# TensorE's semaphore increments in a graph-and-experts kernel: from the matmul itself to a drain behind it

## The reference, cut to what matters

```python
x = layernorm(x)                                  # 6250 x 256
agg_in  = segment_sum((x @ W_in.T + b_in)[src], dst) / max(cnt_dst, 1)
agg_out = segment_sum((x @ W_out.T + b_out)[dst], src) / max(cnt_src, 1)
gi = concat(agg_in, agg_out) @ W_ih.T + b_ih
gh = x @ W_hh.T + b_hh
r, z = sigmoid(gi_r + gh_r), sigmoid(gi_i + gh_i)
n = tanh(gi_n + r * gh_n)
x1 = x_raw + (1 - z) * x + z * n
x2 = x1 + sum over the two best experts of weight * MLP_e(layernorm(x1))
```

## Time and profile before

| | |
|---|---|
| time, median of 3 runs | 3089.86 us (3088.94 to 3093.74) |
| span of the profiled execution | 4434.5 us |
| TensorE matmuls busy in it | 2745.1 us, 62% |
| VectorE, ScalarE, GpSimd busy | 47%, 20%, 49% |
| mean granted TensorE clock | 0.808 of full |

### The profile page before, as it was taken

How to read it: one execution, slowest core, us unless ns; L and a number is a source line. 1 busy time by engine, 2 the same in 40 slices (tenths; PEclk the granted TensorE clock), 3 DMA queues, 4 the chain that set the end, 5 groups by cost and what they waited for, 6 DMA issues and landing times. The chain is left out here.

```text
span 4434.5 us, 68226 instructions
## 1 busy us (share of the span) xinstructions
PE 2745.1 (62%) x14312; PEld 1616.8 (36%) x14313; DVE 2093.1 (47%) x6910; ACT 908.1 (20%) x1572; POOL 2164.5 (49%) x2165
## 2 busy tenths in 40 slices
PE   5211159977777777777764555555555555566896
PEld 2100025533333333333322333333333333345775
DVE  8201179975565556655552333443333433354221
ACT  4100026631112111111110010110111101112443
POOL 0777700035665555655645444444444444433786
PEclk9655589988888888888877777777777777787998
DMA  3100000022222222222222222222222222212444
GB/s 116 30 24 24 18 16 0 0 95 80 86 81 82 78 79 81 79 83 81 84 72 83 77 82 72 74 79 74 83 72 76 75 75 82 71 60 45 80 80 61
DMA packets 178175, 298.24 MB, mean 67 GB/s; under 512 B 51779, under 2 KB 123460, under 8 KB 178118
## 3 DMA queue, kind: packets, MB, share of 16 engines
q0 software_dynamic: 106560, 234.06, 19.8%
q10 hardware_dynamic: 44790, 35.90, 2.6%
q1 hardware_dynamic: 26768, 27.70, 2.0%
HBM read 255.56 MB, written 41.94 MB: 67 GB/s over the span
## 5 line engine op out<-in xcount | busy, mean ns | idle before, releaser
L431 POOL DMA_INDIRECT ring<-split_rows,live x782 | 791.5, 1012 | 923.4 <-DVE live L1035 381.8
L431 POOL DMA_INDIRECT over<-split_rows,gather_row x782 | 747.5, 956 | 933.0 <-PE bank L1674 681.5
L1600 PE MATMUL bank<-over,over 128*128 (+1 forms) x4920 | 1008.9, 354 | 143.1 <-issue 123.6
L1600 PEld LDWEIGHTS bank<-over,over 128*128 (+1 forms) x4920 | 485.9, 102 | 597.7 <-issue 351.9
L974 DVE TENSOR_SCALAR over<-iota_cols,live,live 128x128 f16 x1564 | 411.4, 319 | 119.9 <-issue 113.1
L392 POOL DMA_INDIRECT list<-sort,sort x336 | 332.7, 990 | 218.3 <-issue 111.0
L1674 PE MATMUL bank<-ring,dense 128*128 x980 | 329.5, 430 | 126.7 <-issue 100.1
L1714 PE MATMUL bank<-dense,dense 128*128 128x512 f32 (+1 forms) x600 | 262.0, 437 | 184.5 <-DVE dense L1183 174.1
L1675 PE MATMUL bank<-ones_col,dense 128*128 128x1 f16 x1960 | 334.9, 171 | 2.7 <-issue 2.5
L1674 PE MATMUL bank<-over,dense 128*128 x980 | 277.7, 386 | 94.5 <-issue 77.8
L614 ACT ACTIVATE over<-live,live 128x788 f16 x245 | 221.6, 945 | 492.2 <-remote 271.7
(11 more groups left out here) (304 smaller groups left out, 3927.7 us busy)
## 6 DMA issues: line engine op xcount, KB each, us to landing
norm<-in_x SPq DMA_DIRECT2D x20, 640.0 KB
ring<-split_rows,live POOLq DMA_INDIRECT x782
over<-split_rows,gather_row POOLq DMA_INDIRECT x782
split_rows<-over SPq DMA_DIRECT2D x10, 640.0 KB
in_edge_means<-dense ACTq DMA_DIRECT2D x50, 128.0 KB
dense<-in_x ACTq DMA_DIRECT2D x50, 128.0 KB
dense<-in_edge_means ACTq DMA_DIRECT2D x50, 128.0 KB
out<-dense ACTq DMA_DIRECT2D x25, 256.0 KB
```

The source lines that it names most:

```text
L431: g.indirect_dma_start(out=rings[d][:, i % ring_slots[d], :], out_offset=None, in_=table[:], in_offset=bass.IndirectOffsetOnAxis(ap=gather ...
L1600: ins = t.matmul(bank[h][:, 0:HS + 1], rows_(half), slots(h), start=False, stop=False, skip_group_check=True)
```

## The change

Every increment by TensorE in the ranking, the visits and the dense stage (1386 of them in an execution, by the loops' bounds) used to be carried by the last matmul of a step. It now sits on a separate drain instruction behind that matmul. `slot_done` moves with it: it sat on the last 512-column matmul of a visit and now sits on a drain behind the column of ones that follows; the matmuls stay as they were, in the same order, with the same waits. The increments in the sort loop (`sort_used`), in the folding of weights and in the experts stay on the matmul.

```diff
@@ count_buckets, slot prefix, place_bucket (both loops)
-                    ins.then_inc(S["onehot_used"], 1)
+                    pe.drain().then_inc(S["onehot_used"], 1)
...
-                ins.then_inc(S["slot_prefix_ready"], 1)
+                pe.drain().then_inc(S["slot_prefix_ready"], 1)
@@ visit
                     for q in range(BATCH):
...
-                        summed = t.matmul(sums[k][:, :], oh, rows, start=False, stop=False, skip_group_check=True)
-                        ins = t.matmul(counts[k][:, 0:1], oh, ones_col[:], start=False, stop=False,
+                        t.matmul(sums[k][:, :], oh, rows, start=False, stop=False, skip_group_check=True)
+                        t.matmul(counts[k][:, 0:1], oh, ones_col[:], start=False, stop=False,
                                        skip_group_check=True)
-                        if q == BATCH - 1 and frees:
-                            summed.then_inc(S["slot_done"], BATCH)
+                    if frees:
+                        pe.drain().then_inc(S["slot_done"], BATCH)
                     if d == 0:
                         for i in range(VISIT_TILES):
-                            ins = sort_tile(at_ * VISIT_TILES + (past + i), i, at_)
-                    ins.then_inc(S["node_onehot_used"], 1)
+                            sort_tile(at_ * VISIT_TILES + (past + i), i, at_)
+                    pe.drain().then_inc(S["node_onehot_used"], 1)
@@ end of bucket_sum
                 t.matmul(counts[k][:, 0:1], zeros16[:, 0:P], ones_col[:], start=False, stop=True,
-                         skip_group_check=True).then_inc(S["bucket_done"], 1)
+                         skip_group_check=True)
+                pe.drain().then_inc(S["bucket_done"], 1)
@@ turn_a, turn_b, rz_products, n_products, turn_pair, route, score, ranks, list_tiles: each as here
-                ins.then_inc(S["tile_a_turned"], 1)
+                pe.drain().then_inc(S["tile_a_turned"], 1)
```

More of the change, by code:

```diff
@@ L1734, in turn_b @@
                 pe.wait_ge(S["flags_ready"], r * 2 + (o + 1))
-                t.transpose(turned[:, D:D + P], flags[:].rearrange("p a b -> p (a b)"), ident[:]).then_inc(S["tile_b_turned"], 1)
+                t.transpose(turned[:, D:D + P], flags[:].rearrange("p a b -> p (a b)"), ident[:])
+                pe.drain().then_inc(S["tile_b_turned"], 1)
             order = ((0, 0), (1, 1), (2, 4), (3, 5), (4, 2), (5, 3))
@@ L1749, in rz_products @@
                 if part == 1:
-                    t.matmul(rz_bank[:], flags_T, bias_pack[:, 0:2 * D], start=False, stop=True, skip_group_check=True
-                             ).then_inc(S["rz_summed"], 1)
+                    t.matmul(rz_bank[:], flags_T, bias_pack[:, 0:2 * D], start=False, stop=True, skip_group_check=True)
+                    pe.drain().then_inc(S["rz_summed"], 1)
             def n_products(r, o, part):
@@ L1762, in n_products @@
                     t.matmul(n_bank[:], flags_T, bias_pack[:, 2 * D:G3 + D], start=False, stop=True,
-                             skip_group_check=True).then_inc(S["n_summed"], 1)
+                             skip_group_check=True)
+                    pe.drain().then_inc(S["n_summed"], 1)
             def turn_pair(q):
@@ L1770, in turn_pair @@
                                           xn[:, jj, c * P:c * P + P], ident[:])
-                ins.then_inc(S["xn_turned"], 1)
+                pe.drain().then_inc(S["xn_turned"], 1)
             def route(q):
@@ L1776, in route @@
                     ins = t.matmul(route_bank[:, 0:2 * P], r_w1[:, k, :], xn_T[:, k, :], start=(k == 0), stop=(k == 1))
-                ins.then_inc(S["router_summed"], 1)
+                pe.drain().then_inc(S["router_summed"], 1)
             def score(q):
@@ L1783, in score @@
                                    router_h[:, tt * P:tt * P + P], r_w2[:], start=True, stop=True)
-                ins.then_inc(S["logits_summed"], 1)
+                pe.drain().then_inc(S["logits_summed"], 1)
             def ranks(l):
@@ L1794, in ranks @@
                                    start=False, stop=(tt == 1), skip_group_check=True)
-                ins.then_inc(S["places_summed"], 1)
+                pe.drain().then_inc(S["places_summed"], 1)
             def list_tiles(l):
@@ L1803, in list_tiles @@
                                        stop=False, skip_group_check=True)
-                ins.then_inc(S["list_used"], 1)
+                pe.drain().then_inc(S["list_used"], 1)
             def clear_list():
```

## The result

The changed kernel takes 3920.57 us (median of 4 runs) where the kernel before took 3089.4 us beside it: 1.267 times the time, interval 1.263 to 1.271, 831 us more. The forecast of 3650 us (3230 to 3850) had the direction and the hold of the sequencer right, priced it at full clock, and was 270 us short.

What follows compares the result with a forecast made beforehand. GpSimd's gathers, 978 us per direction, were taken as the bound, TensorE just under. Serialized by drains, TensorE takes over: 378 us more in direction 0, 243 in direction 1, on 3090 gives 3711, less 60: 3650 us (3230 to 3850).

Steps and rivals of the forecast that it cites:

- The late increments: Matmul increments arriving up to some 20 us late in the profile; at most 70 us of the timed run theirs.
- Taking 60 us off the sum: From 3711 us, for moments in the timed 3090 when TensorE was already late, taken as counted in the new totals.
- The rival of a cure: Late increments also slow the timed runs and drains cure them: 3020 to 3080 us, chance 0.07.
- The slack of 48 us in each direction: In the gather stretches, TensorE's work of 930 us against GpSimd's 978 us of gathers.
- A drain holds the sequencer until the array is empty: At each drain TensorE's sequencer loses its lead; loop visits 4.75 us in direction 0; likeliest case, chance 0.55.
- the queued drain: Rival: the drain waits in TensorE's queue while the sequencer runs on, 0.3 us each; 3270 us, chance 0.20.
- the head of the first sorted tile: Direction 0 visits, behind the first drain: sequencer work of 0.25 us, about a third of 0.7 us per tile.
- The dense stage: In direction 1, 328 drains at 0.35 us each add 115 us to TensorE.
- The ranking: 78 drains there, some 0.3 us of delay per group, hide under VectorE's work; 23 us if that cover were gone.
- the prediction's own estimate of 3190 us: Time by the Trainium skill's 175 ns per lone matmul: 1108 drains in the two stretches would cost 194 us.
- The sum for direction 1: TensorE there: 930 + 136 + 40 + 115 = 1221 us, 243 us over GpSimd's 978.
- The rival of the fallen clock: Serial visits drop TensorE's clock to 1.2 GHz for a third of the visits, 310 us more: 3950 us, chance 0.12.

Runs made afterwards that it cites:

- before_again: The kernel before, unchanged, run and profiled a second time: 3095.0 us, ratio 1.001, profiled span 3096.2 us.
- visits0_only: The kernel before with drains in the visits of direction 0 alone, other increments on their matmuls: 3425.4 us, ratio 1.105.
- bare_drain: The kernel before, increments all on their matmuls, plus a drain that carries nothing at the end of each visit: 3499.0 us, ratio 1.128.
- dense_only: The kernel before with drains in the dense stage alone (328), other increments on their matmuls: 3167.7 us, ratio 1.022.
- rank_only: The kernel before with drains in the ranking and slot prefix alone (78): 3108.0 us, ratio 1.0032, 9 us more.
- after_warm: The changed kernel plus three 384-column matmuls of zeros behind the last drain of each loop visit of direction 1: 3717.3 us, ratio 1.197.
- after_tiny: The changed kernel plus three one-column matmuls of zeros behind the last drain of each loop visit of direction 1: 3924.5 us, ratio 1.268.

## Why the prediction was wrong, point by point

**The late increments: right, and the hinge of it.** The account that took 1414 us out of a 4434.5 us profile gave 3020 us, and `before_again` shows the kernel without them at 3096. The 70 us between 3020 and 3090, which had no other name, have one now: the first gather comes at 574, not 558, and the gathers of the two directions take 46 and 36 us more than 978, because a gather lasts 1005 and 991 ns in the mean, not 950; behind them some 24 us are less than in my account. So the 70 us were neither late increments nor moments in which TensorE was late. Taking 60 us off the sum was right all the same, because 1356 and 1221 us already were whole stretches; the reason given for it was not. The rival of a cure is out: no experiment with drains was faster than before.

**GpSimd paces, TensorE close under it: right,** by GpSimd's 8 us of waits. The slack of 48 us in each direction was not: TensorE waits 32 and 80 us for rows. A visit of direction 0 in an undisturbed execution takes 3.63 us, not the 3.04 that I read from one behind a visit at 1.2 GHz, during which the sequencer had gathered a lead; I set one fast visit for all.

**A drain holds the sequencer until the array is empty: right.** The drains' records, `visits0_only` and `bare_drain` show it, and the queued drain is out. Loop visits were forecast at 4.75 and 2.32 us and take 5.06 and, at full clock, 2.43. The term that was short is the head of the first sorted tile, 0.25 us by my estimate: the drain ahead of it costs 0.73 us in all, not 0.45. The bucket's close went the other way: from its last visit's start to the next first visit 6.9 us, forecast 4.3 + 4.3. The two errors cancel, so that 1331 against 1356 us is in part luck.

**The dense stage: right in size, in part by luck.** 115 us for TensorE less its slack of 48 was 65 us, and `dense_only` costs 69, but the slack was larger and the clock lower than this sum has them.

**The ranking: "hides under it": wrong by 9 us** (`rank_only`).

**Two slips in the numbers.** The drains of the two stretches are 1308, not 1108. With that the prediction's own estimate of 3190 us comes to about 3220, and the cure would break even at 0.07 us a drain, not 0.09; neither comes near the measured time. And 3650 + 310 is 3960, not 3950.

**The signs in the profile: mostly there.** The drains' records, the 1.15 us ahead of a visit, 0.59 us (not 0.4) ahead of the sorted tiles. VectorE's L1180, which waited up to 14.2 us before, waits 4.5 us at most for its drain, but `before_again` has no late increments either, so this is no doing of the drains. GpSimd waits for L1678 173 times, for 390 batches not "most". And the span did not fall to some 3700 but to 3916 us.

**The sum for direction 1, "at full clock": the step that failed.** I priced the lost lead with durations of 2.4 GHz and gave the fallen clock 0.12, because between 80 and 111 us a TensorE that is busy half the time keeps a clock of 1.00. In direction 0 that row carried over (0.97 with visits that idle 1.15 and 0.6 us around twelve matmuls in a row). In direction 1 it did not: four pairs, then 1.4 us of nothing, on and on, and the clock stood at 0.72. `after_warm` against `after_tiny` puts 200 us on it. With the clock lifted to 0.92 direction 1 takes 1264 us, 250 over before, where I had 1221, 243 over 978, and the kernel takes 3717 us, 67 us above the forecast of 3650 and inside the range. In that profile the excess over my terms is 43 us in direction 1, 30 between and behind the directions and 25 at the first gather, less 11 in direction 0. The rival of the fallen clock was priced at 3950 us, 30 from the measured time, though by a wrong split: a third of the visits in both directions, where it was 77% of the visits of direction 1 (four pairs that took over 1.1 us from first to last start) and 4% of direction 0. The range ended at 3850 because I cut that rival in half. The Trainium skill's page "TensorE: Matmul & The Clock Gate", section "HAM oscillation — how this bites in real kernels", tells of a kernel whose matmuls come in short bursts with waits for DMA between them, and which pays with a clock that falls again and again. Direction 1 shows the same pattern, with gaps of 1.4 us, shorter than in the page's example, and no DMA behind most of them. I had weighed that page's latency figure (3190 us by it, far off) and not this section.

## What to carry to other kernels

An increment on a drain costs what the sequencer's lead was worth. Before adding one, read what the sequencer does behind it: where loop heads or register work followed, a visit got 0.7 to 0.9 us longer here; in straight matmul code a drain cost 0.2 us of run time, with part of it hidden under the gathers. Then ask what the new idle time does to TensorE's clock, stage by stage and not by one row: a stage of short bursts lost two thirds of its price to the clock. And a profile whose span is far from the timed runs is first to be brought to account against them, and taken again if it can be: its waits may be that execution's own.

## What the runs showed of the hardware that I had not expected

- Work added made a kernel faster: 585 matmuls of zeros took 203 us off 3920, and the same instructions with one column each took nothing off.
- A drain on an empty array has a record of 13 ns but costs about 0.1 us (two of them: 5.06 to 5.25 us per visit).
- Drains that carried nothing, behind increments that had not moved, made the kernel 395 us slower (`bare_drain`).
- In one execution of fourteen profiled ones many semaphore updates of matmuls came late, by up to some 20 us, in stretches where GpSimd issued indirect DMAs, and the span grew from 3096 to 4434 us. What caused it stays open.
